# Causal mask in the first layer: from a matmul into the score bank to a fused VectorE operation per head

## The reference

```
scores = jnp.einsum('bqhd,bkd->bhqk', q, k) * scale
scores = jnp.where(causal[None, None], scores, min_val)
attn   = jax.nn.softmax(scores, axis=-1)
ctx    = jnp.einsum('bhqk,bkd->bqhd', attn, v)
out    = jnp.einsum('bsd,ed->bse', ctx, out_w) + out_b
x      = x + out + ffn(xn)
```

## Time and profile before

| | us |
|---|---|
| median of 3 runs | 1138.77 |
| range of the runs | 1137.49 to 1146.46 |
| profiled execution, its own time | 1142.02 |
| span of the profiled execution | 1140.3 |
| units of layer one, first to last maximum starts | 37.2 to 382.0 |
| PE busy, whole span | 1060.2 (93%) |
| DVE busy, whole span | 838.5 (74%) |
| ACT busy, whole span | 687.9 (60%) |

### The profile page before, as it was taken

One profiled execution on the slowest core, in us unless ns is written; L12 is line 12 of the kernel. 1 busy time (PEld: TensorE's weight loads), 2 busy tenths in 40 slices (PEclk: granted clock), 3 DMA queues, 4 the chain that ended last, 5 costly groups with the idle time before them and its releaser, 6 DMA issues.

```text
span 1140.3 us, 21382 instructions
## 1 busy us (share of the span) xinstructions
PE 1060.2 (93%) x7363; PEld 968.6 (85%) x7363; DVE 838.5 (74%) x1695; ACT 687.9 (60%) x1921; POOL 518.8 (45%) x626
## 2 busy tenths in 40 slices
PE   8778799999699789999999999999999999999996
PEld 7567679778688778888989999999999999899996
DVE  5676677877666676888777777778777777777775
ACT  3676566666556444555566666666666665555553
POOL 4596654755564200004863444544343443588200
PEclk9799999999899999999999999999999999999999
DMA  7656746746654456653534554554555453333120
GB/s 243 163 158 181 192 147 191 195 152 189 173 171 122 142 163 178 206 172 115 190 116 157 152 176 149 163 154 135 151 161 173 144 163 97 107 102 111 57 93 19
DMA packets 140282, 171.71 MB, mean 151 GB/s; under 512 B 11152, under 2 KB 103440, under 8 KB 139152
## 3 DMA queue, kind: packets, MB, share of 16 engines
q1 hardware_dynamic: 137104, 161.96, 47.1%
q0 software_dynamic: 3072, 8.39, 2.2%
HBM read 121.95 MB, written 48.37 MB: 149 GB/s over the span
## 4 chain that ended last, share of the span: by engine, by line
PE 62%; DVE 11%; POOL 7%; DMA 7%; ACT 6%; issue 4%; SPq 3%; DVEq 0%; POOLq 0%; ACTq 0%
PE ps_m L1686 25%; PE ps_s L1686 9%; PE ps_t L1686 6%; PE ps_b L1686 4%; DMA d_w_head<-parts 3%; POOL d_xs L1322 3%; PE ps_b L847 3%; ACT probs L498 3%; DMA d_q_scr<-sT 2%; PE ps_t L1802 2%; PE ps_c L1802 2%; PE ps_c L1686 2%; DVE neg_max L789 1%; PE ps_m L847 1%; PE ps_t L912 1%
## 5 line engine op out<-in xcount | busy, mean ns | idle before, releaser
L1686 PE MATMUL ps_m<-xTa,w_qk 128*128 128x512 f32 x768 | 199.6, 399 | 6.6 <-DMA xTa<-d_xn1T 3.4
L1439 ACT ACTIVATE probs_a<-ps_s,neg_max_a 128x256 f32<-128x256 f32 x256 | 118.0, 473 | 143.6 <-DVE neg_max_a L1652 143.6
L1686 PEld LDWEIGHTS ps_m<-xTa,w_qk 128*128 128x128 f32 x768 | 137.2, 189 | 36.9 <-DVE v L1505 4.6
L498 ACT ACTIVATE probs<-ps_s,neg_max 128x128 f32<-128x128 f32 (+1 forms) x256 | 104.9, 420 | 59.5 <-DVE neg_max L789 58.3
L1652 DVE TENSOR_REDUCE neg_max_a<-ps_s 128x2 f32<-128x512 f32 x128 | 88.1, 691 | 47.2 <-PE ps_s L1686 45.6
L1339 POOL CAST we_down<-raw_down_e 128x256 fp32r<-128x256 f32 x47 | 18.7, 398 | 208.6 <-DMA raw_down_e<-in_we_down 208.6
L1686 PE MATMUL ps_m<-w_v,xTa 128*128 128x256 f32 x768 | 106.1, 287 | 0.0
L1686 PE MATMUL ps_s<-kTa,qTa 128*128 128x256 f32 x768 | 102.8, 283 | 0.8 <-DVE kTa L1475 0.6
L1686 PE MATMUL ps_t<-pTa,v 128*128 128x256 f32 x768 | 103.5, 284 | 0.0
L1686 PEld LDWEIGHTS ps_s<-kTa,qTa 128*128 128x128 f32 x768 | 96.8, 192 | 1.4 <-DVE kTa L1475 1.2
L1686 PEld LDWEIGHTS ps_t<-pTa,v 128*128 128x128 f32 x768 | 97.0, 191 | 0.1
(11 more groups left out here) (257 smaller groups left out, 2845.0 us busy)
## 6 DMA issues: line engine op xcount, KB each, us to landing
w_qk<-d_w_head SPq DMA_DIRECT2D x64, 512.0 KB, 3.9
raw_up<-in_we_up SPq DMA_DIRECT2D x47, 352.0 KB, 3.6
d_w_head<-parts SPq DMA_DIRECT2D x128, 128.0 KB, 2.3
raw_down_e<-in_we_down SPq DMA_DIRECT2D x47, 256.0 KB, 2.7
codes<-in_w_codes SPq DMA_DIRECT2D x64, 128.0 KB
scales<-in_w_scales SPq DMA_DIRECT2D x64, 128.0 KB
q<-d_q_scr SPq DMA_DIRECT2D x32, 256.0 KB, 5.4
d_xs<-zeros SPq DMA_DIRECT2D x16, 384.0 KB, 6.4
```

What stands on the lines that cost most here:

```text
L498: last = act.activation(probs[:, g % 3, a * w:(a + 1) * w], ps_s[g % 2][:, a * w:(a + 1) * w], ACT.Exp, bias=neg_max[:, g % 2, a:a + 1], s ...
L1439: last = act.activation(probs[:, s, t, :], ps_s[s][:, t * SEQ:(t + 1) * SEQ], ACT.Exp, bias=neg_max[:, s, t:t + 1], scale=1.0, accum_out=s ...
L1686: last = pe.matmul(out, lhs[i], rhs[j], start=start and n == 0, stop=stop and n == 2, skip_group_check=True)
```

## The change

The mask product of `scores(g)`, its two casts on ACT and PE's wait for them are gone; the product of q and k starts the bank. On DVE, instead of one maximum per unit, one `tensor_tensor_reduce` per head takes that head's columns of the bank and the mask, writes -(score + mask) back into the bank in place, and gives the minimum of it, which is the negated maximum. The exponential takes scale -1. The mask stays in float32 in SBUF, 256 columns wide, the left half zero and the right half the triangle, so that a head of 256 columns takes all of it and a head of 128 columns the right half. DVE waits once, at unit 0, for POOL's constants. The diff, with declarations of buffers and semaphores cut:

```
         pool.memset(ident[:], 0.0).then_inc(filled, 1)
-        pool.memset(mask_f[:], 0.0).then_inc(filled, 1)
+        pool.memset(mask_wide[:], 0.0).then_inc(filled, 1)
...
-        pool.affine_select(out=mask_f[:], in_=mask_f[:], compare_op=ALU.is_ge, fill=MASKED, base=0,
+        pool.affine_select(out=mask_wide[:, P:2 * P], in_=mask_wide[:, P:2 * P], compare_op=ALU.is_ge, fill=MASKED, base=0,
                            pattern=[[-1, P]], channel_multiplier=1).then_inc(const_ok, 1)
...
                 last = act.activation(probs[:, g % 3, a * w:(a + 1) * w], ps_s[g % 2][:, a * w:(a + 1) * w], ACT.Exp,
-                                      bias=neg_max[:, g % 2, a:a + 1], scale=1.0,
+                                      bias=neg_max[:, g % 2, a:a + 1], scale=-1.0,
                                       accum_out=sums[:, 2 * s + t, h:h + 1])
...
             if item[0] == "q" and item[2] == 0:
-                act.wait_ge(const_ok, 2)
-                act.activation(ident_r[:], ident[:], ACT.Copy).then_inc(consts_r, 1)
-                act.activation(mask_r[:], mask_f[:], ACT.Copy).then_inc(consts_r, 1)
...
             if g < ALL:
                 nh = DC * units[g][4]
+                w = 512 // nh
+                if g == 0:
+                    dve.wait_ge(const_ok, 2)
                 dve.wait_ge(s_full.sem, s_full.at(0, g + 1))
-                dve.tensor_reduce(neg_max[:, g % 2, 0:nh], ps_s[g % 2][:].rearrange("p (h k) -> p h k", h=nh), AX.X,
-                                  ALU.max, negate=True).then_inc(max_ok.sem, 1)
+                for h in range(nh):
+                    at = ps_s[g % 2][:, h * w:(h + 1) * w]
+                    last = dve.tensor_tensor_reduce(at, at, mask_wide[:, 2 * P - w:2 * P], -1.0, 1.0e30, ALU.add, ALU.min, neg_max[:, g % 2, h:h + 1])
+                last.then_inc(max_ok.sem, 1)
...
-            if g == 0:
-                pe.wait_ge(consts_r, 2)
...
-            by_head = out[:].rearrange("p (h k) -> p h k", h=nh)
-            pe.matmul(by_head[:, :, t * P:w], ident_r[:], mask_r[:].unsqueeze(1).to_broadcast([P, nh, P]), start=True, stop=False, skip_group_check=True)
             for a in range(nj):
                 last = pe.matmul(out[:, a * DC * w:(a + 1) * DC * w].rearrange("p (c k) -> p c k", c=DC),
                                  q3[:, s, j + a, t * P:(t + 1) * P], k3[:, s, :, 0:w],
-                                 start=False, stop=(a == nj - 1), skip_group_check=True)
+                                 start=(a == 0), stop=(a == nj - 1), skip_group_check=True)
```

More of the change, by code:

```diff
@@ L96, in stage_layer0 @@
     w_qkv = [sb(f"w_qkv{i}", [P, DC, D + P], R32) for i in range(2)]
-    nc.sbuf_base += 4 * 4 * PC
+    mask_wide = sb("mask_wide", [P, 2 * P])
+    nc.sbuf_base += 4 * (4 * PC - 2 * P)
     parts = [sb(f"parts{i}", [P, 2, PC], R32) for i in range(2)]
@@ L101, in stage_layer0 @@
     probs = sb("probs", [P, 3, 512])
-    ident_r = sb("ident_r", [P, P], R32)
-    mask_r = sb("mask_r", [P, P], R32)
+    nc.sbuf_base += 4 * 2 * P
     region_heads = nc.sbuf_base
@@ L149, in stage_layer0 @@
     raw_up = sb("raw_up_l0", [P, DC, HID], I32)
-    mask_f = sb("mask_f", [P, P])
     assert nc.sbuf_base <= region_probs
@@ L268, in stage_layer0 @@
     filled, const_ok, pads_zero = (sem(n) for n in ("filled", "const_ok", "pads_zero"))
-    qkv_high, qkv_ready, small_ok, consts_r = sem("qkv_high"), sem("qkv_ready"), sem("small_ok"), sem("consts_r")
+    qkv_high, qkv_ready, small_ok = sem("qkv_high"), sem("qkv_ready"), sem("small_ok")
     gate_up_ready, down_ready, late_high, late_ready = sem("gate_up_ready"), sem("down_ready"), sem("late_high"), sem("late_ready")
```

## The result

The changed kernel takes 1151.69 us (median of 4 runs, 1151.24 to 1153.5), the kernel before 1139.44 in the same comparison (4 runs, 1137.49 to 1146.46): ratio 1.010, 95% interval 1.007 to 1.013. That is 12.3 us slower by medians, against a forecast of 14.7. The profiled execution of the changed kernel took 1153.5 us, span 1151.8.

A forecast was written before the change was run, and what follows sets the result against it. Layer one was taken as bound by a chain of waits between DVE and ACT, with ACT waiting for the maximum. Chain growth 14.2 plus off-chain units 4.0 less gain 3.5 gave +14.7, 1153.5 us; range 1137 to 1172.

The forecast's parts named there:

- wrong within 5 us of 384: Sign at layer two's start: the forecast is wrong if it begins within 5 us of 384; 15 us later was expected.
- 85 or more: Sign at ACT's wait for the maximum: it grows from 58 us to 85 or more.
- rival C: PE bounds most layer-one steps, so removed products shorten them: up to 15.0 us faster, to 1123.8; chance 0.08.
- The gain of 3.5 us: Mask products removed from PE: 17 on the chain give 2.7 us, seven more near layer one's end 0.8.
- The accumulator read: On DVE, behind each fused instruction: taken as 0.12 us, the middle of 0.09 to 0.16 on ACT.
- A: Rival for DVE's fused instructions: the accumulator read is free or absent, +0.8 us, 1139.6; chance 0.22.
- 28 maxima: DVE maxima on layer one's chain: 15 long-key ones growing 0.32 us, 13 short-key ones 0.72, 14.2 us in all.
- ten more short-key units: Short-key units off the chain and outside the DMA stretches: 0.40 us charged for each, 4.0 us in all.
- Rival B: DVE's fused instructions and reads do not overlap: 0.62 or 0.49 us per head, +34 us, 1173; chance 0.14.
- Rival D: At the idle gap of 132 to 136 us and the low clock after it, stalls give back 7.4: 1146; chance 0.14.
- The covers: Waits in layer one that hide costs: nine short-key units under DMA stretches cost nothing, 6.5 us if uncovered.
- The casts: Two mask casts removed from ACT: worth nothing, since ACT idles behind them; at most 0.6 us without that wait.

The follow-up runs named there:

- edit 1: Kernel before with the mask product of all 96 units removed and nothing in its place, so the mask is left out: 1141.04 us against 1140.68, ratio 1.000.
- the split maximum: Kernel before with its one maximum per unit cut into one plain maximum per head, mask product kept: 1148.23 us, ratio 1.007.
- the long-key units: Kernel before with the change made in the 64 long-key units only, maximum and product kept in the others: 1147.61 us, ratio 1.005.
- the short-key ones: Kernel before with the change made in the 32 short-key units only, maximum and product kept in the others: 1146.55 us, ratio 1.007.
- busy ahead: Kernel before with an idle DVE memset (300 columns short-key, 60 long-key) in front of each maximum: 1146.04 us, ratio 1.006.
- more ahead: Kernel before with idle DVE memsets of 560 and 220 columns in front of each maximum, on a slower chip: 1180.25 us against 1168.4, ratio 1.009.
- the small dose behind: Kernel before with an idle DVE memset (300 columns short-key, 60 long-key) behind each maximum, after its signal: 1139.9 us, ratio 1.000.
- the large one: Kernel before with idle DVE memsets of 560 and 220 columns behind each maximum: 1147.92 us against 1139.55, ratio 1.006.
- the first pair of memsets: Kernel before with idle DVE memsets of 300 and 60 columns, behind each maximum in one run (1139.9 us), in front in the other (1146.04 us).
- edit 2: Kernel before with the fused instruction per head put in and the mask product kept, so the mask is added twice: 1151.94 us, ratio 1.010.

## Why the prediction was right, and where its terms were off

**Direction and place held.** Layer two has its length and starts 10 to 11 us later (forecast 15; "wrong within 5 us of 384"); ACT's wait for `neg_max` is 85.7 us ("85 or more"); DVE's wait for scores shrank. What the earlier trace rows said, scores early and maximum late, decided it: rival C would have needed the reverse, and edit 1 prices it at 0.

**The gain of 3.5 us did not come** (edit 1: 0.4 slower, interval of 0.2% either way). The step that failed was to read 17 products on the chain as 17 shortened steps. The likely reason, argued and not shown: a product is a link of the chain when PE happens to arrive last; with DVE's queue just behind it, the step is then paced by DVE, and 0.12 us less of PE moves nothing.

**The accumulator read was mis-sized**: 0.12 us taken, from ACT's row. On DVE a row of 139 ns is there, but from start to start, by my estimate, it adds some 0.02 to 0.03 us, (0.12 - 0.08) / 2 and (0.35 - 0.24) / 4: a fused instruction of 256 columns starts its successor after 0.34 or 0.38, one of 128 after 0.20 or 0.25 (0.21 was worked out without a read). So a unit grows by 0.12 and 0.35 and not by 0.32 and 0.72, and DVE's growth is 18.9 us and not 43.5. By the test I had set, "within 0.21, A is right", the price of A (0.08 and 0.24) was nearer to the true one than the forecast's, and its result (+0.8) was wrong by 11 us.

**The share that passes on was mis-sized the other way.** The sum multiplied 28 maxima by growth in DVE's queue and charged ten more short-key units. With the measured growth it gives 15 x 0.12 + 13 x 0.35 = 6.4, and 10 x 0.23 = 2.3 for the ten, less 3.5: +5.2. The quantity that goes with the slip is not the start of DVE's next operation but the end of the last read: 0.18 and 0.42, more than the queue's own growth. With this delay and without the gain, the same 28 maxima give 15 x 0.18 + 13 x 0.42 = 8.2, where the slip is 10.2. Worked out in the same way, after the fact, the other runs with a delay come to 3.5 for the split maximum (slip 4.5), 2.7 for the long-key units (2.5), 5.5 for the short-key ones (5.4), 2.2 for busy ahead (3.8) and 6.7 for more ahead (9.3, on the slower chip). All but the last are within the 2 us by which slips are uncertain, so one chain with the right delay does well here (though four of its 28 maxima stand on it with only 0.08 to 0.29 us, and were counted in full). What it leaves out shows in the two runs without a delay: the small dose behind has -2.0, the large one +4.6. Whether the ten units off the chain cost anything (2.4 by this delay) no run tells.

That delay costs where equal work does not is shown by the first pair of memsets. How much of it passes on is not: by slips it is 41% of the whole delay in the changed kernel, 42 and 40% in the split maximum and the short-key units, but 22% in the long-key units and 70% in busy ahead.

So it was luck that the sum came within 2.4 us of the total: a price two to three times too high met a cost per unit that was counted at the wrong place, and a gain that did not come. The range was right for a weaker reason than the sum suggests.

**Rival B** is out: 0.25 us per short head, not 0.49. Had each fused instruction kept its successor waiting for its whole row, it would have been 0.42 to 0.47 or 0.29 to 0.33 us from start to start; the trace has 0.34 to 0.38 and 0.20 to 0.25. The read itself is there, as an instruction of its own: 256 reads beside 256 fused instructions. It starts 0.34 and 0.38 or 0.20 and 0.25 us behind its fused instruction, together with the next one where that has nothing to wait for.

**Rival D** gives back 0.8 us at its place and not 7.4. The gap went along with the units: PE is idle for most of 137 to 141 us (0.85 us busy), and the 8 us behind it have the granted clock of 0.57 that they had before, so the stretch of lower clock was paid again in full. What a shorter gap would have spared of it, the 3.4 us of the rival, no run shows. Why the gap moved: what DVE waits for in it is an inverse root on POOL, 4.4 us before and 3.5 now, and POOL comes to it only behind weight chunks, the first of which waits for a store to DRAM that follows the stores of q. Start of q's stores, then of that chunk, first before and then changed:

```profile
90.89 2.33 SPq L339 DMA_DIRECT2D d_q_scr<-sT  x4
95.51 2.32 SPq L338 DMA_DIRECT2D d_q_scr<-sT  x4
...
126.54 0.87 POOL L443 TENSOR_TENSOR parts<-codes,scales 128x256 fp32r<-128x256 f32 x1 [5.63 <-DMA d_w_head<-parts]
131.23 0.74 POOL L442 TENSOR_TENSOR parts<-codes,scales 128x256 fp32r<-128x256 f32 x1 [5.14 <-DMA d_w_head<-parts]
```

The DMA stretch begins 4.6 us later and the wait at its end is over 4.7 us later, because the q that opens it comes from the compute side, as the "against" of rival D said; the root follows (133.63 and 138.31), and the stall covers nothing of the slip that came before it. Another 2.6 us come back at the third DMA stretch, and turn 3 loses about 1 us more until its last unit. The forecast had the 14.2 us spread over the whole chain; in fact the slip is at 12.0 by unit 70, late in turn 2, and what comes after adds next to nothing.

**The covers.** That nine short-key units under the three DMA stretches cost nothing, a term of the sum, no run shows; in its place there is the slip of the changed kernel, which falls by 0.8 us at the first stretch and by 2.6 at the third. The casts: edit 2 keeps both, and its time is the changed kernel's, so taking them out gave nothing visible. POOL's wider fill and ACT's scale are in both kernels and were not priced alone; the first maximum starts at 37.3 us against 37.2, and an exponential of 256 columns takes 471 ns against 472.

**What stays open.** The exact share of delay and of work in the 12 us; the place of a large dose; the long-key units' own size, and why layer two took 7 us longer in their profiled execution. A signal per head was not tried: in the long-key unit above the first head's read is over 0.48 us after the start (100.66 + 0.14 - 100.32), the last one 0.86. ACT would then read a bank that DVE is still writing, and what comes of that no run shows.

## What to carry to other kernels

Before splitting a reduction by head, ask which engine waits for its **last** result: look at what is added to the time from the first start to the end of the last instruction, accumulator read included (0.86 and 1.09 us here, where the one maximum took 0.68). Here 10 us of work cost 6 to 7 us ahead of the signal and nothing behind it; for 26 us the two places were not told apart, and the work behind cost 8 as well. Then look whether the operand that is spared on the other engine was ever late: here scores lay ready in 87 of 96 units, and the relief was worth nothing (edit 1: +0.4 us). And price a small delay by that last result and not by the growth of the engine's queue: times the 28 links of the chain it gave 8.2 us where the layer had slipped by 10.2.

## What the runs showed of the hardware

- A fused add and minimum on VectorE with accumulator, 128 partitions, from PSUM and back to PSUM: 443 ns for 256 columns, 319 ns for 128, successor after 0.34 to 0.38 and 0.20 to 0.25 us. Writing the sum back into the bank costs nothing that shows: the addition in the earlier trace rows of the same width that writes to SBUF has the same 0.42 and 0.34 as the first fused instruction of a long-key unit.
- The accumulator read on VectorE has a row of 83 to 146 ns and lies under the next instruction. Where ScalarE waited for the last one, all of its 0.14 us was in the 0.86 and 1.09 us from the first start; from start to start it adds 0.02 to 0.03 us by the estimate above.
- A plain maximum of 512 elements in one instruction is over after 0.68 us, in two after 0.75, in four after 0.87.
- VectorE had 9.9 us more busy time in layer one (a memset of 308 ns behind the maximum of each short-key unit, of 108 ns in each long-key one, partly under their neighbours) at no cost in time; 26.5 us of it cost 8.4.
- The unchanged kernel takes 1139 us on one chip and 1168 on another; so only kernels on the same chip were compared.
